# The other groups' products and the weighted sums of the heads change places on TensorE

## The reference

```
x = x + self_attention(layernorm(x))      # one head; of each row's scores the 32 largest count
x = x + cross_attention(layernorm(x), ctx, ctx)   # 16 heads of 8 features, softmax over 128 keys
x = x + ffn(layernorm(x))                 # 8 experts, each row goes to the one with the largest affinity
```

```
scores  = Q @ K.T / sqrt(8)               # 128 x 128 per head
weights = softmax(scores)
out     = weights @ V                     # the weighted sums: 128 x 8 per head
```

## The kernel before

| half step | `before` | `after` | copied by ScalarE to |
|---|---|---|---|
| 0 | context(e), L1521 | cross_keys(e), L1526 | k_room, L1305 |
| 1 | cross_values(e), L1645 | xn_rows(h), L1521 | self_room (xn_t), L1303 |
| 2 | queries(h), L1526 | probs_rows(e), L1521, and counts | self_room (probs_t), L1303 |
| 3 | attention(e), L1672 | self_scores(h), L1680 | self_room (scores), L1303 |
| 4 | self_values(h), L1690 | feats_rows(f), L1521 | feats_t, L1303 |
| 5 | nothing | nothing | |
| 6 | nothing | xn2_rows(e), L1521, and affinities(f) | xn2_t (ctx_t), L1303 |
| 7 | nothing | cross_queries(e), L1526 | q_room, L1305 |

## Time and profile before

### The profile page before, as it was taken

The page is one execution under the profiler, slowest core; times in us unless marked ns, Lnnn a source line. Parts: engine busy times, 40 slices in busy tenths (PEclk is TensorE's granted clock), DMA queues, the critical chain, the costliest instruction groups (busy, mean ns, idle before and its releaser), DMA issues. The chain is left out here.

```text
span 400.4 us, 11365 instructions
## 1 busy us (share of the span) xinstructions
PE 352.5 (88%) x3499; PEld 248.9 (62%) x3499; DVE 294.2 (73%) x1204; ACT 240.6 (60%) x527; POOL 198.8 (50%) x361
## 2 busy tenths in 40 slices
PE   6988989999999999999998889999989387999990
PEld 5766645555654654664564555555579377999980
DVE  6799846897898899898888876768546255767670
ACT  1464437667676686687576575645447245878750
POOL 4787410320550375276275267573736763544551
PEclk9899969999999999999999999999859978999996
DMA  5515201231231222222211122110143232543110
GB/s 139 158 24 176 52 18 24 52 103 25 51 84 23 52 76 63 50 77 59 51 28 53 26 76 63 27 37 9 55 110 106 96 132 84 153 128 91 32 31 0
DMA packets 30155, 26.96 MB, mean 67 GB/s; under 512 B 5891, under 2 KB 25479, under 8 KB 30096
## 3 DMA queue, kind: packets, MB, share of 16 engines
q1 hardware_dynamic: 26016, 19.59, 18.7%
q0 software_dynamic: 2784, 6.37, 4.6%
q10 hardware_dynamic: 1296, 0.28, 0.5%
HBM read 14.73 MB, written 8.01 MB: 57 GB/s over the span
## 5 line engine op out<-in xcount | busy, mean ns | idle before, releaser
L1013 DVE TENSOR_REDUCE neg_hmax<-s_bank 128x4 f32<-128x512 f32 x128 | 82.1, 684 | 40.8 <-PE s_bank L1568 38.2
L1312 ACT ACTIVATE weights<-s_bank 128x512 f32<-128x512 f32 x128 | 69.9, 596 | 28.8 <-PE s_bank L1586 24.6
L1579 PE MATMUL s_bank<-q_room,k_room 32*128 32x512 f32 x256 | 80.3, 646 | 0.4 <-ACT weights L1312 0.2
L1568 PE MATMUL s_bank<-k_room,q_room 32*128 32x512 f32 x256 | 76.9, 647 | 0.2 <-DVE neg_hmax L1013 0.2
L813 POOL TENSOR_TENSOR x<-x_bv,attended 128x128 f32<-128x128 f32 x32 | 14.6, 455 | 75.9 <-DVE attended L1040 75.9
L475 DVE TENSOR_TENSOR q_room<-s_bank,b_cols 128x512 f32<-128x512 f32 x39 | 27.0, 691 | 27.3 <-PE s_bank L439 15.0
L1610 PE MATMUL pvt_bank<-weights,xv 128*32 128x128 f32 x1024 | 42.6, 284 | 3.5 <-ACT hmax_t L1303 3.2
L439 PE MATMUL s_bank<-q_room,self_room 128*128 128x128 f32 x312 | 45.6, 294 | 0.0
L439 PEld LDWEIGHTS s_bank<-q_room,self_room 128*128 128x128 f32 x312 | 42.2, 210 | 0.0
L824 POOL DMA_INDIRECT routed_rows<-pay,slot x32 | 33.0, 1031 | 12.4 <-issue 7.9
L510 ACT ACTIVATE self_room<-w,gamma_t 128x512 f32 x39 | 28.2, 722 | 15.4 <-PE s_bank L439 9.3
(11 more groups left out here) (214 smaller groups left out, 749.5 us busy)
## 6 DMA issues: line engine op xcount, KB each, us to landing
w<-in_w SPq DMA_DIRECT2D x16, 256.0 KB, 3.9
k_room<-routed_rows SPq DMA_DIRECT2D x31, 130.0 KB
x_in<-in_x SPq DMA_DIRECT2D x8, 256.0 KB, 3.2
ctx_in<-in_ctx SPq DMA_DIRECT2D x8, 256.0 KB, 3.0
k_room<-k_room SPq DMA_DIRECT2D x128, 16.0 KB
q_room<-q_room SPq DMA_DIRECT2D x112, 16.0 KB
routed_rows<-blank SPq DMA_DIRECT2D x9, 130.0 KB
q_room<-routed_rows SPq DMA_DIRECT2D x8, 130.0 KB
```

Of the source, the lines that this page charges most:

```text
L1013: dve.tensor_reduce(neg_hmax[:, first:first + 4], bank.rearrange("p (h k) -> p h k", k=S), AX.X, ALU.max, negate=True).then_inc(s["s1_max" ...
L1312: act.activation(weights[:, u, :], s2_bank[:, (u % 2) * GS:(u % 2 + 1) * GS], ACT.Exp, scale=HEAD_SCALE).then_inc(s["s2_exp"], 1)
L1568: pe.matmul(s1_bank[:, (u % 2) * GS:(u % 2 + 1) * GS], natural(q_nat, g, j, strip(u)), masked(k_masked, K_RING, g, j, strip(u)), start=Tru ...
L1579: pe.matmul(s2_bank[:, (u % 2) * GS:(u % 2 + 1) * GS], natural(k_nat, g, j, u), masked(q_masked, Q_RING, g, j, u), start=True, stop=False)
```

## The change

In each half step the two `pv` calls are issued ahead of `after()`, not behind it. The weighted sums of the last half step of all (`g == NG - 1 and n == 7`) stay behind it. Only TensorE's order changes; the numbers of products, the semaphores and the orders of the other engines are the same.

```
                     if scores_first:
                         keep_awake(6)
-                    after()
                     if has_c and u == 2:
                         pv(g, j, 0)
                         pv(g, j, 1)
                     if has_c and u == 0 and G * g + j > 0:
                         pv(*following(g, j, -1), 2)
                         pv(*following(g, j, -1), 3)
+                    after()
                     if g == NG - 1 and n == 7:
                         pv(g, j, 2)
                         pv(g, j, 3)
```

## The result

The changed kernel takes 416.89 us (416.02, 416.83, 416.96, 416.99) against 401.82 (399.67 to 404.51, four runs): ratio 1.038, with an interval of 1.0329 to 1.0431. 415 was predicted. Some executions of a kernel fall into a slower state whatever its order, and the ratios in this document leave them out. Its profiled execution took 416.02 us with a span of 414.3, so 13.9 more than the span before, where the steps of the prediction add up to 11.8.

The account below looks back on a forecast made before the run. TensorE sets the pace (busy 29.47 of 31.40 us a group); 1.9 + 2.4 + 1.35 + 3.3 + 3.3 - 0.45 = 11.8 us on 402.1 gives 413.9, a median of 415. Own range 413 to 417, widened to 408 to 419.

Parts of the forecast that it names:

- What releases a copy: At the boundaries: product or exponentials, whichever ends last, releases ScalarE's copy; the consumer's delay is the product's less the slack.
- Rival 1: Exponentials release the copies, so product and `pv` swap for free and only gains stay: 2.4 us faster, 400.9; 5 in 100.
- Keys, 1.9: Half step 0 to 1: no slack, cross_values 0.57 later in three groups, 0.1 for each of two others; 1.9 us.
- xn_t, 2.4: Half step 1 to 2: slack 0.19, so 0.47 in four groups, 0.5 in the first; 2.4 us together.
- probs_t, 1.35: Half step 2 to 3: slack 0.30, so 0.27 in five groups and 0 in the sixth; 1.35 us.
- Scores and the queries' projection, 3.3 each: Half steps 3 to 4 and 7 to 0: no slack, 0.66 in five groups at each boundary; 3.3 us each.
- Half steps 4 to 6: 0: Boundaries 4 to 5, 5 to 6, 6 to 7: 0; the 0.27 delay at 4 to 5 is given back two half steps on.
- Gains, -0.45: In the last two groups `pv` fills feats_rows' wait for ScalarE's normalisation: 0.2 each, -0.45 us, ends 0 and -1.1.
- The rule of the Trainium skill: Half steps 0 and 2: one tile-shape change fewer; 11 boundaries saving a drain each, about 1.0 us, sum 10.8 not 11.8.
- Rival 2: VectorE sets the pace in half steps 4 to 7, so the 3 to 4 delay vanishes: 8.5 us, 412; 10 in 100.
- Rival 3: TensorE's clock falls to 1.2 GHz now and then, twice in the run: 7 us more, 422; 5 in 100.
- feats_t: Half step 4 to 5: copy 0.27 later, taken as 0, with 0 and 4 x 0.27 = 1.1 us as ends.

Follow-up runs that it names:

- halves of the change: Two kernels: `pv` ahead of `after` in even half steps only, or odd ones only, against the kernel before: ratios 1.0112 and 1.0273.
- the even kernel: `pv` ahead of `after` in the even half steps only, against the kernel before: 399.56 against 396.87 us, ratio 1.0112.

## Why the prediction was right, and where its steps were off

- **What releases a copy: right.** The copies of keys, scores and the queries' projection start 0.10 us after their products with ScalarE idle ahead of them (that of xn_t 0.03 after its transposes), and the losses of the halves of the change add to the whole. Rival 1 is out: nothing comes for free at 0 to 1, 3 to 4 and 7 to 0.
- **Keys, 1.9: right for the trace that it was read from, 0.5 short for the next.** Second to fifth turn: 0.58, 0.58, 0.57 and 0.08 in the first pair of profiles, so 1.8, as said. The fifth was put at 0.1 because its keys' product waited 0.42 for the context's copy. In the second profile of the kernel before that wait isn't there, and the turn loses its 0.57: 2.3. What had been read as a property of the turn came and went between runs.
- **xn_t, 2.4 against 2.7.** The first turn's 0.5 was 0.55. In the fourth turn, the one that the slack was read from, the loss is the 0.47 of the prediction, partly by luck: the transposes take 0.06 more behind `pv`, and the slack was 0.07 more than put down, since their copy starts 0.03 and not 0.10 behind them. In the second, third and fifth it is 0.56, since in the kernel before that piece is 0.10 shorter there (4.38 against 4.48): one turn had been taken for four.
- **probs_t, 1.35 against 1.0.** The slack was 0.37 and not 0.30: the copy starts 171.94 - (171.25 + 0.66) = 0.03 behind these transposes, and I had put the 0.10 of the scores there.
- **Scores and the queries' projection, 3.3 each: the mechanism right, the size 0.1 too small a turn.** I priced the change of tile shape once (0.09, attended_rows to `pv`). The product behind `pv` pays again: 1.16 against 1.06. Before, that second change lay between product and consumer, in a stretch that was waiting anyway; now it stands on the path. 0.77 a turn, five turns, twice: 7.7 in place of 6.6.
- **Half steps 4 to 6: 0, right.** Those half steps hold no loss in the turns without a meeting: the last piece, from self_values to the next context, is 0.76 longer, which half step 7 accounts for. `pv` of half step 5 waits 0.64 for hmax_t in place of 0.44, and the first two instructions of S1 in half step 7 take 0.77 in place of 0.97: the delay is given back as said.
- **The cast beside GpSimd's sum: no term at all.** 1.1 us over the third and fourth turn (0.68 and 0.40 above 0.77), 1.9 with the late copy in the first profile. It could have been looked for: VectorE's cast was through 0.6 us ahead of a GpSimd instruction of 1.27 us, and I asked of VectorE only whether it would set the pace.
- **Gains, -0.45: not seen.** The wait for feats went from 2.4 to 1.0 as predicted, but the stretch behind the fifth turn is the same in the two profiles of the result. The second profiles, 184.1 and 181.3 us there, differ by more than any gain that was put down. It is below what can be told.
- **The rule of the Trainium skill, TensorEngine Tiling (Array Packing), Tiling Modes,** by which the even half steps would save a drain each: the even kernel lost 0.57 and 0.20 where the rows of `pv` gave 0.57 and 0.27, so no saving of 0.09 shows at the keys. The change of shape that went away lay between keys and `pv`, ahead of a consumer that waits. That is only the argument; no run takes it by itself.
- **Rival 2** is out: half step 3 alone makes a turn 0.77 longer, and nothing behind it in the turn gives that back. **Rival 3** is out in the loop's full turns (1.00 in both windows), and over the whole run the mean granted clock was 0.953, against 0.949 before.

12.25 - 0.45 was the sum. The boundaries gave 13.7 without the meeting, the meeting 1.1, the gains nothing: 14.8. The boundaries were put too low, one term was missing, and the range held since its upper end had been put for others (feats_t, the keys in full). That 415 lies within 2 us of 416.89 is partly luck: it was counted from the 403.26 known then, and the kernel before measured 401.82 in the result, so the forecast's 11.8 stands against 15.1 between the medians.

## What to carry to other kernels

Between the end of a product and the start of the one that reads its evacuated copy lie 0.75 us at the scores, 0.84 at the keys and 0.89 at the context, of which the copy itself is 0.60 or 0.69. Independent work that stands there is free as long as it fits in; the same work ahead of the product costs its length at every turn, less the time that the copy would have been held by something else. Before moving a filler, ask of each neighbour what it covers: attended_rows covered the copy of the maxima, and VectorE waited for them, so they could go in one half step of four and not in the others. When one engine's order is delayed and another's isn't, look for VectorE's short instructions that come to lie beside a long one of GpSimd, and compare their distance with the delay: 0.6 us between them was not enough for a delay of 0.77.

## What the runs showed of the hardware that I had not expected

- A cast of 128x16 on VectorE that lasts 0.17 us elsewhere takes 1.29 beside a GpSimd sum of 1.26 us, and a subtraction of 128x16 1.19 in place of 0.17. In these rows it ends within 0.04 us of GpSimd's instruction; GpSimd's isn't longer. Beside another GpSimd instruction (L899, 128x4, 1.04 us) the cast took its 0.17.
- A product behind one of another tile shape takes 0.06 to 0.10 us more (1.16 against 1.06, 1.12 against 1.02, 0.66 against 0.60).
- At the end of the loop the granted clock differs between runs although TensorE is nearly always busy. The second profile of the kernel before, and then the kernel with attended_rows late in half step 7:

```profile
288.00:292.00 4.00, 3.90 (x43) 2.28 (x43) 2.53 (x17) 1.45 (x4) 3.43 (x7) 1.00 0.22 78
```

```profile
284.00:288.00 4.00, 3.54 (x40) 2.03 (x37) 0.55 (x2) 1.47 (x3) 2.54 (x5) 0.50 0.34 80
```

  The kernel before itself had 0.50 there in its first profile and 1.00 in its second, so 1.2 or 2.4 GHz at the same place of the same kernel. Of 23 executions of the kernel before in one session, from 390.05 to 399.42 us, the shortest has the highest mean clock (0.975) and those of 399.12 and 399.17 the lowest (0.946), but 398.51 has 0.956 and 393.23 has 0.958: the clock goes with a part of the spread. How large a part, and what decides it, is open.
